# Score strips in the order sibling, own, and one DMA transpose per token block instead of two

## The reference

```python
xn = _layernorm(x)                                   # x is (4, 2048, 2048)
q, k, v = heads(xn @ Wq + bq), heads(xn @ Wk + bk), heads(xn @ Wv + bv)   # 16 heads of 128
scores = einsum('bhqd,bhkd->bhqk', q, k) / sqrt(2048)
attn = softmax(where(causal, scores, -inf))          # over 2048 keys
out = einsum('bhqk,bhkd->bhqd', attn, v)
x = x + (out @ Wp + bp) + moe(xn)                    # 2 shared and 16 routed experts
```

## Time and profile before

| | us |
|---|---|
| device time, median of 2 runs | 5378.66 (5272.03 and 5485.28) |
| the profiled execution, its own device time | 4873.61 |
| its span on the slowest core | 4872.1 |
| spans of the eight cores | 4857.4 to 4872.1 |
| TensorE busy (matmul) | 3835.1 (79%) |
| VectorE busy | 1142.2 (23%) |
| ScalarE busy | 871.4 (18%) |

### The profile page before, as it was taken

One profiled execution on the slowest core, in us unless ns is written; L12 is line 12 of the kernel. 1 busy time (PEld: TensorE's weight loads), 2 busy tenths in 40 slices (PEclk: granted clock), 3 DMA queues, 4 the chain that ended last, 5 costly groups with the idle time before them and its releaser, 6 DMA issues.

```text
span 4872.1 us, 49771 instructions; the slowest of 8 cores (4857.4 to 4872.1 us)
## 1 busy us (share of the span) xinstructions
PE 3835.1 (79%) x18201; PEld 1837.5 (38%) x18520; DVE 1142.2 (23%) x1731; ACT 871.4 (18%) x1341; POOL 137.5 (3%) x240
## 2 busy tenths in 40 slices
PE   0035646666475765599999999999999999999997
PEld 0022424234242432244444444444444444444443
DVE  2323333333433233311111111111111111111111
ACT  1224233232423324011000110011000110001100
POOL 0000000000000000000000000000000000000000
PEclk9997868778687877699999999999999999999999
DMA  4433241322323232234345343443434434344434
GB/s 94 99 75 55 47 72 36 57 46 45 67 39 68 36 58 43 43 66 84 63 74 95 65 79 65 78 86 65 79 74 78 78 72 74 74 85 71 79 67 121
DMA packets 336345, 335.16 MB, mean 69 GB/s; under 512 B 304721, under 2 KB 305105, under 8 KB 311249
## 3 DMA queue, kind: packets, MB, share of 16 engines
q0 software_dynamic: 68544, 241.19, 27.7%
q1 hardware_dynamic: 266420, 82.39, 8.6%
q10 hardware_dynamic: 1152, 8.39, 0.4%
HBM read 499.69 MB, written 8.39 MB: 104 GB/s over the span
## 4 chain that ended last, share of the span: by engine, by line
PE 73%; DMA 12%; DVE 5%; SPq 4%; issue 3%; ACT 2%; DVEq 0%; another core or an unknown queue 0%; ACTq 0%; POOL 0%; POOLq 0%
PE psF L959 28%; PE psF L924 14%; PE psF L917 13%; DMA atT<-prob 9%; PE psF L592 5%; PE psF L557 5%; PE psF L782 4%; SPq L749 3%; DVE acc L854 3%; PE psF L619 2%; DMA xstage<-xin 1%; PE psF L878 1%; DVE bno L317 1%; DMA lofm<-lobf 1%; PE psF L837 1%
## 5 line engine op out<-in xcount | busy, mean ns | idle before, releaser
L959 PE MATMUL psF<-w2b,hbuf 128*128 128x512 bf16 x6209 | 1363.5, 379 | 32.1 <-ACT hbuf L938 25.5
L924 PE MATMUL psF<-xnf_own,w1b 128*128 128x512 bf16 x3168 | 1201.6, 379 | 7.0 <-issue 0.3
L917 PE MATMUL psF<-xnf_own,w1b 128*128 128x512 bf16 x3041 | 1153.8, 379 | 0.0
L959 PEld LDWEIGHTS psF<-w2b,hbuf 128*128 128x128 bf16 x6336 | 618.5, 98 | 777.1 <-issue 33.6
L976 DVE SCALAR_TENSOR_TENSOR acc<-psF,gat,acc 128x512 f32<-128x512 f32 x512 | 384.2, 750 | 2072.0 <-PE psF L959 2055.8
L938 ACT ACTIVATE hbuf<-psF,b1t 128x512 bf16<-128x512 f32 x396 | 250.4, 683 | 2537.0 <-PE psF L917 2300.4
L782 PE MATMUL psF<-atT,vbuf 128*128 128x256 bf16 x832 | 180.2, 406 | 445.5 <-DMA atT<-prob 445.5
L917 PEld LDWEIGHTS psF<-xnf_own,w1b 128*128 128x128 bf16 x3168 | 310.2, 98 | 376.0 <-issue 2.6
L924 PEld LDWEIGHTS psF<-xnf_own,w1b 128*128 128x128 bf16 x3168 | 310.2, 98 | 374.1 <-issue 1.1
L782 PEld LDWEIGHTS psF<-atT,vbuf 128*128 128x128 bf16 x832 | 113.3, 142 | 528.9 <-issue 483.6
L709 DVE TENSOR_REDUCE amx<-scob 128x1 f32<-128x1152 f32 (+7 forms) x128 | 232.9, 1819 | 32.5 <-ACT scob L698 18.7
(11 more groups left out here) (77 smaller groups left out, 1633.3 us busy)
## 6 DMA issues: line engine op xcount, KB each, us to landing
w2b<-wstream POOLq DMA_DIRECT2D x72, 1408.0 KB, 13.6
w1b<-wstream POOLq DMA_DIRECT2D x90, 1024.0 KB, 8.2
xstage<-xin SPq DMA_DIRECT2D x16, 1024.0 KB, 6.9
w1b<-wstream POOLq DMA_DIRECT2D x18, 512.0 KB, 7.7
wrA<-wstream POOLq DMA_DIRECT2D x16, 512.0 KB, 5.0
wrB<-wstream POOLq DMA_DIRECT2D x16, 512.0 KB, 5.2
wvb<-wstream POOLq DMA_DIRECT2D x8, 1024.0 KB, 8.0
y<-acc ACTq DMA_DIRECT2D x8, 1024.0 KB, 11.7
```

What stands on the lines that cost most here:

```text
L917: mm0 = T(lambda t_, dc=dc, fci=fci, wslot=wslot, ps=ps0: t_.matmul(ps[:], w1b[:, wslot, dc, fci * 128:(fci + 1) * 128], xnf_own[:, dc, 0: ...
L924: mm1 = T(lambda t_, dc=dc, fci=fci, wslot=wslot, ps=ps1: t_.matmul(ps[:], w1b[:, wslot, dc, fci * 128:(fci + 1) * 128], xnf_own[:, dc, 51 ...
L959: mm = T(lambda t_, fc=fc, tcq=tcq, wslot=wslot, ps=ps: t_.matmul(ps[:], hbuf[:, fc, tcq * 128:(tcq + 1) * 128], w2b[:, wslot, fc, :], sta ...
```

## The change

In `plan_scores` the two sibling tiles now come first, in banks 0 and 1 and in columns 0 to 1023 of the strip, and the own tiles follow in banks 6, 7, 0 and so on, in columns from 1024 on. The row maximum and the exponential read the same number of columns as before. Since a strip is now one run of (tc+9)*128 columns whose first 1024 are always the sibling's, one DMA transpose of tc+9 blocks (L747 of the new kernel) fills slots 0 to tc+8 of `atT`. The matmuls of L782 (L771 of the new kernel) read the slots by the new numbering; their order and number stay. The streams dsa and dsb aren't used in this stage any more.

```diff
@@ plan_scores: the sibling tiles move to the front
+                SROT = (0, 1, 6, 7)
+                for j in range(2):
+                    bk = SROT[j]
+                    ps, pb = psF[bk], B_("ps%d" % bk)
+                    mm = T(lambda t_, j=j, tc=tc, ps=ps: t_.matmul(
+                        ps[:], qbuf[:, tc * 128:(tc + 1) * 128],
+                        kbuf[:, 1024 + j * 512:1536 + j * 512], start=True, stop=True),
+                        wait=qb.r() + kb.r() + pb.w())
...
+                    te = A(lambda a, j=j, sl=sl, ps=ps: a.activation(
+                        scob[:, sl, j * 512:(j + 1) * 512], ps[:],
+                        AF.Identity, scale=SCALE, bias=msk8[:, 0:1]),
+                        wait=[mm] + B_("msk8").r() + (scold if j == 0 else []))
...
-                    bk = SROT[i % 4]
+                    bk = SROT[(2 + i) % 4]
...
-                            scob[:, sl, a0:a1], ps[:, 0:a1 - a0], SCALE, None,
-                            ALU.mult), wait=[mm] + (scold if i == 0 else []))
+                            scob[:, sl, 1024 + a0:1024 + a1], ps[:, 0:a1 - a0],
+                            SCALE, None, ALU.mult), wait=[mm])
...
@@ plan_transposes: one transpose for two
-                    out=atT[:, 0:tc + 1, pos * 128:(pos + 1) * 128],
-                    in_=prob[:, sl, 0:(tc + 1) * 128].rearrange(
-                        "p (c x) -> p c x", c=tc + 1),
+                    out=atT[:, 0:tc + 9, pos * 128:(pos + 1) * 128],
+                    in_=prob[:, sl, 0:(tc + 9) * 128].rearrange(
+                        "p (c x) -> p c x", c=tc + 9),
                     transpose=True),
                     wait=[tnm_tok[tc]] + wv.w())
                 wv.did_w(t1)
                 pr.did_r(t1)
-                t2 = DMA("sync", strm2, lambda s, tc=tc, sl=sl, pos=pos, LA=LA:
-                         s.dma_start(
-                    out=atT[:, 8:16, pos * 128:(pos + 1) * 128],
-                    in_=prob[:, sl, LA:LA + 1024].rearrange(
-                        "p (c x) -> p c x", c=8),
-                    transpose=True),
-                    wait=[tnm_tok[tc]])
-                wv.did_w(t2)
-                pr.did_r(t2)
...
@@ plan_av
-                    slot = 8 + i if reg == "sib" else i
+                    slot = i if reg == "sib" else 8 + i
```

More of the change, by code:

```diff
@@ L649, in plan_scores @@
                 L = LA + 1024
-                atiles = [(a0, min(a0 + 512, LA)) for a0 in range(0, LA, 512)]
                 sc = B_("scob%d" % sl)
@@ L654, in plan_scores @@
                 sc.rdd = {}
+                SROT = (0, 1, 6, 7)
[6 more added lines that the diff above has]
+                        wait=qb.r() + kb.r() + pb.w())
+                    pb.wrd = {}
+                    pb.rdd = {}
+                    pb.did_w(mm)
+                    kb.did_r(mm)
+                    qb.did_r(mm)
+                    te = A(lambda a, j=j, sl=sl, ps=ps: a.activation(
+                        scob[:, sl, j * 512:(j + 1) * 512], ps[:],
+                        AF.Identity, scale=SCALE, bias=msk8[:, 0:1]),
+                        wait=[mm] + B_("msk8").r() + (scold if j == 0 else []))
+                    pb.did_r(te)
+                    B_("msk8").did_r(te)
+                    sc.did_w(te)
+                atiles = [(a0, min(a0 + 512, LA)) for a0 in range(0, LA, 512)]
                 lastev = None
-                SROT = (0, 1, 6, 7)
                 for i, (a0, a1) in enumerate(atiles):
-                    bk = SROT[i % 4]
+                    bk = SROT[(2 + i) % 4]
                     ps, pb = psF[bk], B_("ps%d" % bk)
@@ L662, in plan_scores @@
                         kbuf[:, a0:a1], start=True, stop=True),
-                        wait=qb.r() + kb.r() + pb.w())
+                        wait=pb.w())
                     pb.wrd = {}
@@ L670, in plan_scores @@
                         te = V(lambda v, a0=a0, a1=a1, sl=sl, ps=ps: v.tensor_scalar(
-                            scob[:, sl, a0:a1], ps[:, 0:a1 - a0], SCALE, None,
-                            ALU.mult), wait=[mm] + (scold if i == 0 else []))
+                            scob[:, sl, 1024 + a0:1024 + a1], ps[:, 0:a1 - a0],
+                            SCALE, None, ALU.mult), wait=[mm])
                     else:
                         te = A(lambda a, a0=a0, a1=a1, sl=sl, ps=ps: a.activation(
-                            scob[:, sl, a0:a1], ps[:, 0:a1 - a0], AF.Identity,
-                            scale=SCALE), wait=[mm] + (scold if i == 0 else []))
+                            scob[:, sl, 1024 + a0:1024 + a1], ps[:, 0:a1 - a0],
+                            AF.Identity, scale=SCALE), wait=[mm])
                     pb.did_r(te)
@@ L680, in plan_scores @@
                 tdg = V(lambda v, tc=tc, sl=sl: v.tensor_tensor(
-                    scob[:, sl, tc * 128:(tc + 1) * 128],
-                    scob[:, sl, tc * 128:(tc + 1) * 128],
+                    scob[:, sl, 1024 + tc * 128:1024 + (tc + 1) * 128],
+                    scob[:, sl, 1024 + tc * 128:1024 + (tc + 1) * 128],
                     dgm[:], ALU.add), wait=[lastev] + B_("dgm").r())
@@ L685, in plan_scores @@
                 B_("dgm").did_r(tdg)
[L686 to L704, removed]
                 am = B_("amx%d" % sl)
@@ L745, in plan_transposes @@
                 pr = B_("prob%d" % sl)
-                LA = (tc + 1) * 128
                 strm = "dta" if tc % 2 == 0 else "dtb"
-                strm2 = "dsa" if tc % 2 == 0 else "dsb"
                 t1 = DMA("sync", strm, lambda s, tc=tc, sl=sl, pos=pos: s.dma_start(
-                    out=atT[:, 0:tc + 1, pos * 128:(pos + 1) * 128],
-                    in_=prob[:, sl, 0:(tc + 1) * 128].rearrange(
-                        "p (c x) -> p c x", c=tc + 1),
+                    out=atT[:, 0:tc + 9, pos * 128:(pos + 1) * 128],
+                    in_=prob[:, sl, 0:(tc + 9) * 128].rearrange(
+                        "p (c x) -> p c x", c=tc + 9),
                     transpose=True),
```

## The result

| | before | after |
|---|---|---|
| device time, median | 5069.39 us (10 runs, 4869.34 to 5485.28) | 4962.68 us (11 runs, 4790.92 to 5418.50) |
| the profiled execution | 4873.61 us | 4780.79 us |
| span of the slowest core | 4872.1 us | 4778.9 us |

The ratio of the times is 0.9821, with a 95% interval of 0.979 to 0.9852: the change makes the kernel 1.8% faster, 87 us on 4870. Executions of either kernel come in two kinds, one several per cent longer at a lower clock, and the two runs that were shown ahead of the prediction were both of the longer kind; the ratio leaves that kind out.

The account below looks back on a forecast made before the run. Transpose landings and issues in attention, 603 us of its chain, were taken as the bound the change touches. Merging 74 plus collisions 12 gave 86 us off the 5378.7 us median: 5293 us, range 5190 to 5385.

Parts of the forecast that it names:

- The pair becomes one transpose: In attention, merging each block's two transposes saves 4.6 us per head, 74 us over 16 heads, at 0.15 us per block.
- The bounds from stage 0: Stage 0's 16-block transposes, 4.2 us quiet to 5.5 us worst, bound the merging between 81 us gained and 13 us lost.
- The collisions with the loads: In odd heads, blocks 4 and 5 lose less time beside the loads of L823: 12 us, from 8 to 52.
- Sibling tiles first: In attention's scores, the new tile order costs 0, at most 0.55 us per head, 9 us.
- What is late next: Scaled `prob` against the previous block's landing in attention: a tie at block 1, 0.5 us of slack at block 5.
- More falls away with the loads: Rival, chance 0.26: blocks 4 and 5 both escape the loads and the slope is lower; gain 133 us, 5246 us.
- The softmax takes over: Rival, chance 0.10: VectorE's or ScalarE's queue delays attention's odd blocks, losing 32 us; gain 54 us, 5325 us.
- The long transposes are dear: Rival, chance 0.06: attention's 16-block transposes cost 5.5 us, so the kernel is 13 us slower, 5392 us.
- The whole fixed price goes: Rival, chance 0.03: each removed attention transpose saves its full issue-to-landing price, at least 2.2 us; gain 196 us, 5183 us.

## Why the prediction was right and where it was wrong

**The predicted time, 5293 us with a range of 5190 to 5385, was wrong**: the median is 4963. The step that failed is the last of the sum, "The runs shown have a median of 5378.7, 10% above it ... so I take the difference over": I took the median of two runs for the scale of the kernel. In ten runs the median is 5069, 309 us lower, and four of the ten lie at 4869 to 4897, beside the profiled execution of 4873.6 that I had in hand. With 5069 in its place the sum would have given 4983, and its term for the gain was right. On the profile's own scale I had 4788 us, and the profiled execution is 4780.8. The 86 us that I took off are 1.8% of 4873.6; I wrote 1.6%, since I divided by 5378.7. The measured 1.8% is 87 us.

**The sum holds, term by term.**

- "*The pair becomes one transpose*", 0.15 us per block from 3.25 to 4.30: measured 3.22, 3.34, 3.50, 3.66, 3.85, 3.99, 4.15, 4.30. A head has 30.0 us instead of the forecast 30.2, and 16 heads gain 77 us instead of 74. The bounds from stage 0 were right at their quiet end. What the prediction says beside it, that in block 7 at about 210 GB/s "the transfer itself is the limit", does not hold as it stands: block 5 of the odd head was moved at 280 to 291 GB/s once the loads were through. So 210 is not the most that a transpose is moved at, and no run shows what sets it.
- "*The collisions with the loads*", 12 us: the landings and issues on the chain were 603 us. My 557 for the undisturbed pairs held 6 us of the 0.05 us pieces, which the chain counts apart, so the lateness was 603 - 551 = 52 us and not the 46 that I wrote. After the change it is 521 - 480 = 41, so 11 us are gained. The 12 was a pick from 8 to 52, and that it came within 1 us is partly luck. It went as forecast in the head shown: block 4 at 3.85 us, block 5 with the end of the loads. Together it is 88 us, against 86.5 within the attention of the slowest cores and 88.6 in the mean of all.
- "*Sibling tiles first*", 0: ratio 0.9989 when it is done alone.
- "*What is late next*", a tie at block 1 and 0.5 us at block 5: measured 0.08 and 0.54, and the kernel without the landing wait gained 24 us, not 128.

**The rivals.** "More falls away with the loads" asked for block 5 to escape as well; it took 8.4 us. "The softmax takes over" didn't happen in the changed kernel, and is the next bound in the one without the landing wait. "The long transposes are dear" needed 5.3 us for 16 blocks; it was 4.30. "The whole fixed price goes" needed 196 us; 88 were gained, and swapping the pair saved 56 us with no transpose removed, so that it is the offset that counts. The Trainium skill's page "DMA: Bandwidth & Descriptors" (section "Anatomy of one DMA") gives a fixed cost of about 2 us for a DMA that GpSimd issues. The first transposes of the pairs, which SyncE issues, took 2.2 us at the least, near that figure, but in a pair most of it lay beneath the other's.

## What to carry to other kernels

Where transfers of one step are issued back to back, the step costs the issues ahead of the last one plus that one's landing, provided that the others have landed by then. So merge them, and where that can't be done put the longest first: here the swap alone brought two thirds of the gain without a change of layout. The two loads cost the chain 4.4 to 4.8 us per head in each of the three places where they met it, and some 10 us on the odd-numbered cores in one of them; look for a tile that is free earlier instead of delaying the loads. And before a difference is carried to a median of two runs, hold that median against the profiled execution: here it lay 10% above it.

## What was not expected of the hardware

- A transpose issued together with loads from GpSimd's queue took longer than one issued in their midst: 9.1 us on core 4 and 15.0 on core 5 for 16 blocks, against 8.4 for 14. In the same head cores 1, 3 and 7 took 13.6 to 14.4 us and cores 0, 2 and 6 took 9.0 to 9.5. The cause stays open.
- SyncE's issue itself becomes longer in the midst of the loads: the issues of the changed kernel's transposes took 1.38 us in the median, but 4.34 at block 5 of the odd head shown (it began at 870.58, and the merged row of the two ends at 866.67 + 8.26 = 874.93) and 4.59 at most. With the loads laid elsewhere the longest was 1.92. A transpose can be late without it, though: the 14.95 us of block 7 began with an issue of 1.4 us.
- A transpose was moved at about 210 GB/s when it ran undisturbed, but at 280 to 291 GB/s in the last slices of block 5, which had waited behind the loads. What sets the 210 stays open.
